# Paired last pixel chunks, a packed convolution, early text loads and finer steps of the maximum and the moments, with a new order and new banks

## What is computed

```python
h = leaky_relu(batchnorm(conv2d(x, stem_w, stem_b, 4)))
h = leaky_relu(batchnorm(deform_conv(h, conv2d(h, off_w, off_b, 4), dcn_w, dcn_b)))
h = concatenate([h as 25 tokens, txt])
h = h + attention(layernorm(h))       # integer softmax, max and sum over each row of scores
h = h + gelu(layernorm(h) @ w_in + b_in) @ w_out
```

## Time and profile before

| | |
|---|---|
| median of three runs | 1103.54 us |
| the profiled execution, its own time | 1104.14 us |
| its span, first to last instruction | 1102.4 us |
| granted TensorE clock, mean | 0.918 of full |
| PE busy | 922.1 us (84%), 5666 matmul instructions |
| DVE busy | 945.4 us (86%), 1913 instructions |
| ACT busy | 791.9 us (72%), 1841 instructions |
| POOL busy | 295.2 us (27%), 243 instructions |

### The profile page before, as it was taken

One profiled execution on the slowest core, in us unless ns is written; L12 is line 12 of the kernel. 1 busy time (PEld: TensorE's weight loads), 2 busy tenths in 40 slices (PEclk: granted clock), 3 DMA queues, 4 the chain that ended last, 5 costly groups with the idle time before them and its releaser, 6 DMA issues. The chain is left out here.

```text
span 1102.4 us, 18651 instructions
## 1 busy us (share of the span) xinstructions
PE 922.1 (84%) x5666; PEld 569.5 (52%) x5666; DVE 945.4 (86%) x1913; ACT 791.9 (72%) x1841; POOL 295.2 (27%) x243
## 2 busy tenths in 40 slices
PE   3669498989979898989979897988989898986547
PEld 1245245556655645555655645555655646454334
DVE  3867999999999999999989999999999999985850
ACT  2335778777787968788777969788787969575742
POOL 5022323142323332142313232132414233120300
PEclk9979698999989898999989999999989898897768
DMA  6000212212040222222040312222040312213020
GB/s 161 23 27 7 63 30 56 49 46 52 10 88 15 67 38 63 43 51 49 12 87 11 74 32 63 41 51 51 10 89 10 74 31 51 41 39 62 7 56 12
DMA packets 128848, 50.75 MB, mean 46 GB/s; under 512 B 102983, under 2 KB 127726, under 8 KB 128654
## 3 DMA queue, kind: packets, MB, share of 16 engines
q1 hardware_dynamic: 128750, 49.57, 21.1%
HBM read 19.82 MB, written 6.24 MB: 24 GB/s over the span
## 5 line engine op out<-in xcount | busy, mean ns | idle before, releaser
L530 POOL TENSOR_TENSOR m_sb<-mx_sb,a_sb 128x1020 f16<-128x1020 f16 x64 | 134.8, 2106 | 300.0 <-DVE mx_sb L907 300.0
L1092 PE MATMUL bank<-hats_sb,ht_sb 126*96 126x400 f32 (+1 forms) x512 | 200.1, 523 | 2.7 <-DVE hats_sb L830 2.7
L669 ACT ACTIVATE ee_sb<-ee_sb,rs_sb 128x102 f32<-128x102 f32 x640 | 179.8, 367 | 21.3 <-DVE rs_sb L963 21.2
L1209 PE MATMUL bank<-w_out_sb,ge_sb 128*102 128x192 f32 x768 | 164.8, 373 | 23.8 <-DVE y_sb L1006 21.4
L1209 PEld LDWEIGHTS bank<-w_out_sb,ge_sb 128*102 128x102 f32 x768 | 142.8, 195 | 46.6 <-issue 38.6
L538 POOL TENSOR_TENSOR rstd_sb<-ve_sb,half_sb 102x4 f32<-102x4 f32 x32 | 47.2, 1475 | 354.5 <-DVE ve_sb L853 354.5
L1092 PEld LDWEIGHTS bank<-hats_sb,ht_sb 126*96 126x96 f32 (+1 forms) x512 | 74.9, 165 | 98.5 <-issue 94.8
L830 DVE TENSOR_TENSOR hats_sb<-hats_sb 126x1600 f32<-126x1600 f32 x64 | 116.4, 1819 | 0.3
L595 ACT ACTIVATE hats_sb<-bank 126x400 f32<-126x400 f32 x256 | 107.4, 513 | 0.0
L1043 PE MATMUL bank<-xc_sb,stem_w_sb 49*96 49x441 f32 x128 | 46.5, 767 | 70.4 <-DMA xc_sb<-x_col 66.9
L520 POOL TENSOR_TENSOR rx_sb<-offs_sb,mask_sb 96x400 bf16<-96x400 bf16 x64 | 78.0, 1220 | 83.8 <-PE bank L1083 82.5
(11 more groups left out here) (156 smaller groups left out, 1743.3 us busy)
## 6 DMA issues: line engine op xcount, KB each, us to landing
xc_sb<-x_col SPq DMA_DIRECT2D x32, 165.4 KB, 3.5
out<-y_sb SPq DMA_DIRECT2D x32, 153.0 KB
xa_sb<-txt SPq DMA_DIRECT2D x16, 231.0 KB
xr_sb<-txt SPq DMA_DIRECT2D x16, 231.0 KB
q_sb<-qb_sb SPq DMA_DIRECT2D x192, 12.8 KB, 1.9
tok_scratch<-tokb_sb SPq DMA_DIRECT2D x16, 75.0 KB
xa_sb<-tok_scratch SPq DMA_DIRECT2D x16, 75.0 KB
xr_sb<-tok_scratch SPq DMA_DIRECT2D x16, 75.0 KB
```

What stands on the lines that cost most here:

```text
L530: nc.gpsimd.tensor_tensor(M16[b][:], MX[b][:].unsqueeze(2).to_broadcast([128, RT, TOK]), A16[b][:], ALU.subtract).then_inc(m_done, 1)
L669: last = nc.scalar.activation(EE[b][:, r, :], EE[b][:, r, :], ACT.Ln, scale=RS[b][:, r:r + 1])
L1092: last = mm(bank[t.banks[0]][0:C1, 0:SMP], HT[0:rows, t.i, j, :], HATS[b][0:rows, 1 + j, :], start=(j == 0), stop=(j == NCH - 1))
L1209: last = mm(bank[t.banks[0]][0:TOK, 0:D], GE[:, f, t.i * TOK:(t.i + 1) * TOK], WOUT[:, f, :], start=(f == 0), stop=(f == FT - 1))
```

## The change

Six things change together.

1. **Paired last chunks.** The images of odd number in a group lay their last chunk of 63 pixels at partitions 64 to 126 (`SHIFT` = 1 zero column ahead of `H`, 127 rows of hats, constants `LXC`, `LYC` in two forms). The last chunk of an even image is multiplied together with that of the following odd one, in two matmuls of 63 rows on the two halves of the array into two banks; so an even image's sum is complete only in the turn of the odd one. There are four buffers of hats in place of two.
2. **Packed convolution.** The last 4 of the 16 taps are copied by three transfers from 96 partitions of SAMP into the free 32 partitions at the other 12 taps (new SP stage SD), so that 12 matmuls of 128 rows and one of a single row for the bias take the place of 16. The weights' factor is multiplied in by POOL once, in place of DVE.
3. **Text first.** LA starts the text transfer before it waits for the stored tokens; LR too issues text first.
4. **The maximum as three stages** MAX, MXB, MXC, which the table can set apart.
5. **The moments as turns**: `bn_stats` per image (LS1, LS2), one stage with four `bn_aggr` (LN1, LN2), and one addition of epsilon for all four (VE1, VE2).
6. **New tables** `SLOT` and `BANKS`.

```diff
-dve.SUM.10 act.DCN.8 pe.LN1X.15 dve.RCP.10 act.PR.15 dve.EP.9 pe.HTT.9 dve.PW.11 act.SQ.13
+dve.LN2X.12 act.SQ.12 pe.LN1X.15 dve.QQ.11 dve.MAX.10 act.HTT.5 pe.PV2.19 dve.QQG.11 sp.PT.18
...
             def load_tokens(t):
                 n = t.count(GRP)
-
-
+                if t.n >= 1:
+                    sp.wait_ge(xh_done, t.count(GRP, 0))
+                load_text(n, XA, xa_in)
                 sp.wait_ge(tok_out, t.count(16, 16))
-                tokens_of(n, XA, xa_in)
+                load_convolved(n, XA, xa_in)
...
+            def pack_samples(t):
+
+                sp.wait_ge(samp_done, t.count(GRP, GRP))
+                for b in range(C1 // 32):
+                    sp.dma_start(SAMP[C1:128, REST * b:REST * (b + 1), :, :].rearrange("c k g p -> c (k g p)"),
+                                 SAMP[32 * b:32 * b + 32, PACKED:TAPS, :, :].rearrange("c k g p -> c (k g p)")).then_inc(rest_in, 16)
...
+            def fold_taps():
+                pool.wait_ge(prep, BN2_STEPS)
+                nc.gpsimd.tensor_tensor(WD[:], WD[:], inv2.unsqueeze(1).to_broadcast([128, PACKED, D]),
+                                        ALU.mult).then_inc(wd_ready, 1)
...
-                pool.wait_ge(ve_done, t.count(2, 2))
+                pool.wait_ge(ve_done, t.count(1, 1))
...
             def hats(t):
-                b = t.i % 2
-                if t.n >= 2:
-                    act.wait_ge(samp_full, t.count(1, -1))
+                odd = t.i % 2
+                rows = odd * SHIFT + CH
+                if t.n >= GRP:
+                    act.wait_ge(samp_full, t.count(1, 1 - GRP))
...
             def fold_bn2():
                 dve.wait_ge(wd_in_s, 16 * DCN_LOADS)
-                then(v.tensor_tensor(inv2[:], inv2[:], gam2[:], ALU.mult))
-                then(v.tensor_tensor(WD[0:C1, :, :], WD[0:C1, :, :], inv2[0:C1, :].unsqueeze(1).to_broadcast([C1, TAPS, D]), ALU.mult))
...
-            def moments(t, x, x_ready, st, mv, ve, st_done, mv_done, ve_done, xh_done, rstd_s):
-
+            def moments(t, st, mv, st_done, mv_done, xh_done):
+
+                dve.wait_ge(st_done, t.count(GRP, GRP))
+                if t.n >= 1:
+                    dve.wait_ge(xh_done, t.count(GRP, 0))
                 for i in range(GRP):
-                    x_ready(t, i)
...
+                    v.bn_aggr(mv[:, i, :], st[:, i, :]).then_inc(mv_done, 1)
+
+            def image_moments(t, x, st, st_done, mv_done):
+                if t.n >= GRP:
+                    dve.wait_ge(mv_done, t.of_group(GRP, 0))
+                v.bn_stats(st[:, t.i, :], x).then_inc(st_done, 1)
...
+            def variance(t, mv, ve, mv_done, ve_done, rstd_s):
+                dve.wait_ge(mv_done, t.count(GRP, GRP))
+                if t.n >= 1:
+                    dve.wait_ge(rstd_s, t.count(1, 0))
+                v.tensor_scalar(ve[:], mv[:, :, 1], LN_EPS, None, ALU.add).then_inc(ve_done, 1)
...
-                    dve.wait_ge(half_done, t.count(2, 0))
+                    dve.wait_ge(quarter_done, t.count(1, 0))
+                v.tensor_tensor(MA[:], A16[b][:, :, 0:52], A16[b][:, :, TOK - 52:TOK], ALU.max).then_inc(half_done, 1)
+
+            def quarter_max(t):
+                dve.wait_ge(half_done, t.count(1, 1))
+                if t.n >= 1:
                     dve.wait_ge(mx_done, t.count(1, 0))
...
+                v.tensor_tensor(MB[:], MA[:, :, 0:26], MA[:, :, 26:52], ALU.max).then_inc(quarter_done, 1)
+
+            def last_max(t):
+                dve.wait_ge(quarter_done, t.count(1, 1))
+                v.tensor_reduce(MX[t.i % 2][:], MB[:], AX.X, ALU.max).then_inc(mx_done, 1)
...
             def interpolate(t):
...
+                free.take(t, odd, samp_done, 1)
+                dst = bank[t.banks[odd]][0:C1, 0:SMP]
+                if odd:
+                    mm(bank[t.banks[0]][0:C1, 0:SMP], HT[0:LAST, t.i - 1, NCH - 1, :], HATS[t.i - 1][0:LAST, NCH, :],
+                       start=False, stop=True).then_inc(samp_full, 1)
+                    mm(dst, HT[64:64 + LAST, t.i, NCH - 1, :], HATS[t.i][64:64 + LAST, NCH, :], start=True, stop=False)
+                for j in range(NCH - 1):
+                    last = mm(dst, HT[0:rows, t.i, j, :], HATS[t.i][0:rows, 1 + j, :],
+                              start=(j == 0 and not odd), stop=(j == NCH - 2 and odd == 1))
...
                 pe.wait_ge(samp_done, t.count(GRP, GRP))
+                pe.wait_ge(rest_in, t.count(48, 48))
                 free.take(t, 0, tok_done, 1)
                 dst = bank[t.banks[0]][0:GRP * POS, 0:D]
-                for k in range(TAPS):
-                    rows = slice(0, C1 + 1 if k == 0 else C1)
-                    last = mm(dst, SAMP[rows, k, :, :].rearrange("c g p -> c (g p)"), WD[rows, k, :],
-                              start=(k == 0), stop=(k == TAPS - 1))
+                mm(dst, onesq[0:1, 0:GRP * POS], dcnb[:], start=True, stop=False)
+                for k in range(PACKED):
+                    last = mm(dst, SAMP[:, k, :, :].rearrange("c g p -> c (g p)"), WD[:, k, :],
+                              start=False, stop=(k == PACKED - 1))
```

More of the change, by code:

```diff
@@ L32 @@
 SMP = TAPS * POS
+PACKED = TAPS * C1 // 128
+REST = TAPS - PACKED
 ROWS = 6
@@ L36 @@
 LAST = NPIX - 3 * CH
+HALF = CH // 2
+SHIFT = 64 - HALF
 D, TXT = 192, 77
@@ L229, in build @@
         WOUT = sb("w_out", [128, FT, D])
-        LXC, LYC = sb("lx", [3 * NOFF + 3, CH], bf16), sb("ly", [3 * NOFF + 3, CH], bf16)
+        LXC, LYC = ([sb(f"l{a}{odd}", [3 * NOFF + 3, odd * SHIFT + CH], bf16) for odd in range(2)] for a in "xy")
         mask = sb("mask", [3 * NOFF, TAPS], bf16)
@@ L254, in build @@
         RX = [sb(f"rx{b}", [3 * NOFF + 3, TAPS, POS], bf16) for b in range(2)]
-        HATS = [sb(f"hats{b}", [CH, 1 + NCH, SMP]) for b in range(2)]
-        SAMP = sb("samp", [C1 + 1, TAPS, GRP, POS])
+        HATS = [sb(f"hats{i}", [SHIFT + CH, 1 + NCH, SMP]) for i in range(GRP)]
+        SAMP = sb("samp", [128, TAPS, GRP, POS])
         TOKB = sb("tokb", [GRP * POS, D])
@@ L568, in pixels_first @@
                     act.wait_ge(samp_full, t.count(1, 1 - GRP))
-                nc.scalar.activation(HT[:, t.i, :, :].rearrange("p j c -> p (j c)"),
-                                     bank[t.banks[0]][0:CH, 0:NCH * C1], ACT.Copy).then_inc(ht_done, 1)
+                rows = t.i % 2 * SHIFT + CH
+                nc.scalar.activation(HT[0:rows, t.i, :, :].rearrange("p j c -> p (j c)"),
+                                     bank[t.banks[0]][0:rows, 0:NCH * C1], ACT.Copy).then_inc(ht_done, 1)
             def tap_quarters(t):
@@ L720, in _ @@
             dve.wait_ge(inv_full, 1)
-            rows = bank[0][0:SROWS, 0:3 * C1]
-            then(v.tensor_tensor(inv1[:], rows[:, 0:C1], gam1[:], ALU.mult))
+            rows = bank[0][:, 0:3 * C1]
+            then(v.tensor_tensor(inv1[:], rows[0:SROWS, 0:C1], gam1[:], ALU.mult))
             then(v.tensor_tensor(shift1[:], bm1[:, 1, :], inv1[0:1, :], ALU.mult))
@@ L727, in _ @@
             then(v.tensor_copy(W1[64:65, :], W1[0:1, :]))
-            then(v.tensor_copy(inv2[:], rows[0:C1 + 1, C1:3 * C1]))
+            then(v.tensor_copy(inv2, rows[:, C1:3 * C1]))
             def sampling_constants():
@@ L1085, in interpolate @@
             def interpolate(t):
-                b = t.i % 2
+                odd = t.i % 2
+                rows = odd * SHIFT + CH
                 pe.wait_ge(w_done, t.count(1, 1))
                 pe.wait_ge(ht_done, t.count(1, 1))
-                free.take(t, 0, samp_done, 1)
-                for j in range(NCH):
-                    rows = CH if j < NCH - 1 else LAST
-                    last = mm(bank[t.banks[0]][0:C1, 0:SMP], HT[0:rows, t.i, j, :], HATS[b][0:rows, 1 + j, :],
-                              start=(j == 0), stop=(j == NCH - 1))
```

227 lines of the change are left out of this document (110 added, 117 removed).

## The result

The changed kernel takes 1068.6 us (median of four runs, 1065.0 to 1071.5) against 1105.6 (1103.5 to 1111.9): a ratio of 0.963 [0.958, 0.967], 37 us faster. It lies within my range of 1054 to 1114, but I had forecast a gain of 18, so the sum leaves half of it unexplained. The profiled execution took 1071.5 us, its span 1069.7.

What follows compares the result with a forecast made beforehand. VectorE, 93% busy in the middle, was taken as the bound. Terms -15 - 6 - 12 - 6 + 10 + 16 - 2 - 1 = -16 took 1104 to 1088; two more off for overlapping waits gave 1086 us, range 1054 to 1114.

Steps and rivals of the forecast that it cites:

- once: Once-only work: line 740's 3.36 us go from VectorE to POOL against six small steps (-2); run's end one moments step less (-1).
- PE (projection wait): PE 2.3 us per group shorter by pairing and convolution; half of VectorE's projection wait goes: -6 us (0 to -14).
- Moments: In the two layer norms, separate statistics and aggregates take 1.55 us against 1.75 per step: -6 us, between 0 and -10.
- Waits that grow: Before the second norm's first normalised image, VectorE waits 0.6 us more per group for POOL's answer: +10 us (0 to +19).
- The maximum: Setting VectorE's three maximum steps apart turns gaps into overlaps, 0.24 us per image: -15 us (ends -15 and 0).
- Text first: Loading XA's text ahead of the store's landing cuts VectorE's token wait by 0.75 us per group: -12 us (0 to -15).
- Being held: VectorE instructions held beside POOL's products and masks, 4.7 us per group against 3.9, taken as +1.0: +16 us (-44 to +66).
- The sign that I had named: In the profile after, excess times of former lines 929 and 903 sum to about the same, the clip's mean up.
- the other sign: The longest time of the hats' products would tell whether exponentials, with two SBUF inputs, are held too; no size given.
- PE as the pace: Rival: PE was the true pace, so growing terms do not appear and the rest of PE's wait goes: 1054 us, chance 0.15.
- Held time giving all back: Rival: maximum steps meet masks and products, held time rises by 2 rather than 1 us per group: 1102 us, chance 0.18.
- ScalarE's queue: Rival: 9.2 us between two squares make VectorE wait up to 2.8 us a group: 1107 to 1128 us, chance 0.18.

Runs made afterwards that it cites:

- the place alone: Changed kernel with its own moments instructions, but each norm's four statistics standing together right in front of the four aggregates: 1086.8 us, ratio 0.979.
- pixels first: Kernel before, with SP issuing the pixel loads ahead of the store of the convolved tokens and the text's reload: 1095.3 us, ratio 0.991.
- pixels late: Changed kernel with the pixel loads issued behind the transposing transfer of the next image's probabilities, some 7 us later: 1145.3 us, ratio 1.035.
- the run with the exponentials ahead of the bound: Changed kernel with text late and POOL's mask behind the product (1059.7 us), plus an image's exponentials moved ahead of the bound of the next but one: 1058.8 us.
- the run with sixteen products: Changed kernel with the convolution's one-row bias product made four times, so 16 products per group instead of 13: 1068.0 us, ratio 0.966.

## Why the prediction was off by half

Per group, forecast and measured (waits of a stretch divided by its periods):

| step of the prediction | forecast | measured |
|---|---|---|
| maximum, moments, once: VectorE's busy time without what is held | -1.4 | -1.3 |
| text first (token wait) | -0.75 | -0.95 |
| PE (projection wait) | -0.4 | -0.84 |
| wait for the power | +0.6 | -0.34 |
| held by POOL, with the bound's wait | +1.0 | -0.7 held, +1.84 wait |
| the exponentials' wait for squares | 0 | -0.51 |
| scores, queries, probabilities: waits for ScalarE | 0 | +1.09 |
| unlisted small waits | 0 | -0.5 |

(The -0.7 is the change of mean duration, times four images, summed over the halvings, quotients, bounds, remainders, power bits, both steps of the probabilities, exponentials and both normalisations, in six periods from 400 us on; over the whole run the same lines give -12 us, divided by 16 -0.8. The -1.3 is the rest of VectorE's 56.7 to 54.7.) The forecast's lines add up to -1.0 us per group, the measured ones to -2.2, of the 2.25 by which the period shrank.

Two steps failed, and they concern one place. The first is "Moments ... -6 us; between 0 and -10": undoing it costs 27 us. Its working counted the wrong thing. By the instructions, 1.75 us against 1.55, two steps a period differ by 0.4 us, and with the step joined the busy time rises by even less, 0.2. Not counted was that the four statistics of each norm left the front of the chain that begins with its aggregates: 18 us for the place alone, some of it by way of the clock. I priced an order by its instructions, where the order's worth is which chain they delay.

The second is "Waits that grow", +10 us: the wait for the power went down, over the whole run from 22.9 to 15.7 us, in front of the second norm's images from 14.8 to 1.1. It rested on "POOL's answer takes 2.1 us". That was no fixed time. GpSimd's power took 1.90 us before, beside the hats on VectorE, and takes 1.01 where only a cast of 0.26 us stands beside it. From 150 to 950 us the second norm's power took 1.90 us in every group before and 1.01 after; the first norm's went the other way, from 1.17 to 1.71:

```profile
519.88 1.90 POOL L538 TENSOR_TENSOR rstd_sb<-ve_sb,half_sb 102x4 f32<-102x4 f32 x1 [14.30 <-DVE ve_sb L853]
```
```profile
517.46 1.01 POOL L565 TENSOR_TENSOR rstd_sb<-ve_sb,half_sb 102x4 f32<-102x4 f32 x1 [25.09 <-DVE ve_sb L889]
```

So the answer comes 1.1 us behind the addition, and the clip in front of the first image waits 0.80 for its scores in that time anyway; part of the old wait has only changed its name (the row of waits for ScalarE, +1.09). Forecast +10 and measured -7 make 17 us, which is the largest gap in the account by waits on the side of the gain; the 21 us of the moments are the largest by undoing. The two are not to be added, since undoing the moments brings 6 us of that wait back, and the undone parts together exceed the gain.

A rival for the missing half is left open, PE's clock. In the kernel after, a period with a mean clock of 0.94 is 1.8 us longer than the mean of those at the upper level, and the one with 0.97 is 0.7 longer. If it cost the same before, where 10 of 13 periods have 0.94 or 0.95 and three 0.97, the clock would be some 14 of the 37 us. That is an estimate from the periods of after. Before, the three periods with 0.97 (61.5 to 62.2 us) are no shorter than the others (60.6 to 62.2), so it may be much less, and no run holds the clock still.

The maximum: right. 15 us of overlap was the forecast; joined, VectorE has 1.2 us more per period, and 12 us remain after the shorter wait for the product. The trace shows that this wait (I had it in "the bound, which needs the product itself: 1.4") is 1.78.

Text first: the wait went as forecast (-0.95 for -0.75), but that was luck, since its cause was wrong. I read `<-txt` as the text's transfer being late; the row names the transfer that landed last, and that was issued behind the store of tokens which PE finished late. Text first is worth 0 after and 2 us before; pixels first alone 11.

PE: "The 4.46 us that PE stands before the stem ... lies behind the tokens' store in SP's queue both before and after" fails twice. In the new order the stem comes behind the output products of three of the four images of a group, and the pixels have landed; and the stand was not free, since it made the tokens late and the clock fell in it. How much of the 37 us is its doing can't be isolated in the kernel after: pixels late cost 77, more than the gain. The pairing itself is worth 11 rather than a part of 6, PE's shorter convolution 0 to 4, so the two together are not far from my bound of 14. The Trainium skill, TensorEngine Tiling (Array Packing), Key Properties, says that a change of tiling mode drains the TensorE. The pair's 0.85 us agree with the sum made without a price for it.

Being held: the sum was right, the places were not. Forecast +16 us; over the run the bound's wait is 26.7 and the held lines lost 12, together +14. The clip that I named is not held (0.41 us at 526.04, beside a product), the third normalised image is, and the wait for the product is longer than I had it, so errors cancelled. The sign that I had named failed: the excess of the two lines 929 and 903 over their shortest was to stay about the same, and it fell from 44 us to 8. The longest of the hats' products, the other sign, tells nothing: behind the fill they take 1.80 to 1.83 us, before and after.

The rivals. PE as the pace was half right: half of VectorE's extra work was hidden before, all of it counts after. Held time giving all back did not come, and ScalarE's queue had room.

What stays open: how much of the 37 us is the clock's, and what the 37 us would be made of in an order fitted to each part, since the undone parts add to more than the whole.

## What to carry to other kernels

Price a moved instruction by the chain in front of which it stood, not only by its duration: eight statistics of 0.26 us per group, 2 us, were worth 18 us over 16 groups with VectorE's busy time all but unchanged. Read the granted clock of each stretch before counting a stand of PE: what comes behind it can run at the lower level. When a row says that a load was waited for, follow what released its issue before crediting an edit of the load; a one-line move in the old kernel tells. About a microsecond of PE's work per group costs 11 us in one place and 0 to 4 in another, so ask of each edit which wait follows it. And a wait for GpSimd, filled with an instruction that GpSimd's work holds, only changes its name.

## What the runs showed of the hardware

Instructions on f32 are held while GpSimd works as well: the normalisation takes 2.00 us instead of 0.37 and ends 0.1 us behind the product. The exponentials that begin in the product's last microsecond take 1.95 instead of 1.27 (the run with the exponentials ahead of the bound). The f32 reduction stays at 1.20 to 1.22 in all its 64 records. The Trainium skill, SBUF — State Buffer, Who interferes with whom, says that an instruction with two SBUF inputs contends with a GpSimd one that reads SBUF and that a reduction on this chip never contends; for the exponentials, the remainder and the reduction the trace agrees. GpSimd's product itself takes 1.88 to 2.61 us; one of the longest began at 525.60, while VectorE's remainder ran (525.44, 0.68 us), so the holding goes both ways, and GpSimd's small power (102 x 4) takes 1.01 or 1.90 us by what stands beside it. A one-row product with 192 columns takes about as long as one of 128 rows (0.19 and 0.17 us, in the run with sixteen products). Where the granted clock is at its lower level, four records of 128 rows and 408 columns take 3.06 us instead of 1.56. A stand of PE of 4.1 to 5.0 us for its pixels was followed by that level in all 12 groups between 180 and 900 us of the kernel before.
